# A mixture-of-experts stage on one core: each expert's weights in one transfer in place of two

## The reference

```python
x = x + xattn(layernorm(x), ctx_2048, ...)
h = layernorm(x)
w, sel = top_4(softmax(h @ gate_w.T))          # w made to sum to 1
cw_large[t, sel] += w;  cw_small[t, sel // 2] += w
large = sum_e (silu(h @ Wg[e]) * (h @ Wu[e]) * cw_large[:, e]) @ Wd[e]
small = the same with cWg, cWu, cWd, cw_small
x = x + large + 0.05 * small
```

## Time and profile before

| | |
|---|---|
| median of 3 runs | 1032.56 us (1029.6 to 1033.31) |
| the profiled execution | 1028.99 us, its span 1027.2 us |
| PE busy | 973.1 us, 95% of the span |
| DVE, ACT, POOL busy | 551.2, 313.3 and 299.5 us |
| down product y_ps (L1695) | 213.7 us |
| gate and up, g_ps and u_ps (L1678) | 183.2 and 181.4 us |
| adds into out_x (L1531) | 124.9 us on POOL |
| bytes moved | 168.51 MB, mean 164 GB/s |
| granted clock of PE, mean | 0.977 of full speed |

### The profile page before, as it was taken

How to read it: one execution, slowest core, us unless ns; L and a number is a source line. 1 busy time by engine, 2 the same in 40 slices (tenths; PEclk the granted TensorE clock), 3 DMA queues, 4 the chain that set the end, 5 groups by cost and what they waited for, 6 DMA issues and landing times.

```text
span 1027.2 us, 18902 instructions
## 1 busy us (share of the span) xinstructions
PE 973.1 (95%) x5188; PEld 624.8 (61%) x5189; DVE 551.2 (54%) x1382; ACT 313.3 (31%) x632; POOL 299.5 (29%) x397
## 2 busy tenths in 40 slices
PE   8789999999999898489999999999999999999995
PEld 6557676676666555356666666666666666666662
DVE  5677777777767736944443434444443444444341
ACT  2245455555545554921111111111111111111111
POOL 3011101010111001233444344343444434343433
PEclk9999999999999999669999999999999999999998
DMA  6163144241323017348887998989888899889654
GB/s 225 38 170 79 59 103 104 65 111 56 89 68 94 25 48 292 129 101 201 223 237 184 273 249 222 254 219 254 211 216 222 224 244 262 217 213 258 129 110 83
DMA packets 102683, 168.51 MB, mean 164 GB/s; under 512 B 15536, under 2 KB 65840, under 8 KB 98288
## 3 DMA queue, kind: packets, MB, share of 16 engines
q1 hardware_dynamic: 36624, 103.11, 31.6%
q0 software_dynamic: 17872, 43.58, 22.8%
q10 hardware_dynamic: 48144, 21.25, 7.6%
HBM read 101.56 MB, written 29.36 MB: 127 GB/s over the span
## 4 chain that ended last, share of the span: by engine, by line
PE 55%; DMA 1%; issue 0%; ACTq 0%; ACT 0%; POOL 0%; DVE 0%; POOLq 0%
PE y_ps L1695 19%; PE g_ps L1678 17%; PE u_ps L1678 16%; PE at_ps L1687 2%; DMA out_x<-yb,yidx 0%; DMA xg<-xd,tok 0%; ACTq L1557 0%; POOL out_x L1531 0%; PE xt_ps L1663 0%; ACT yb L1568 0%; ACT xT L1578 0%; ACT sg L1562 0%; DVE a L1631 0%; DVE a L1633 0%; POOLq L1539 0%
## 5 line engine op out<-in xcount | busy, mean ns | idle before, releaser
L1695 PE MATMUL y_ps<-W,aT 128*128 x468 | 213.7, 592 | 0.2 <-issue 0.2
L1531 POOL DMA_INDIRECT out_x<-yb,yidx x78 | 124.9, 1601 | 252.7 <-ACT yb L1568 129.5
L519 DVE TENSOR_REDUCE mx<-s 128x2 f32<-128x512 f32 x256 | 163.4, 682 | 59.2 <-PE s L710 58.5
L1678 PE MATMUL g_ps<-W,xT 128*128 x624 | 183.2, 437 | 0.9 <-ACT xT L1578 0.9
L398 ACT ACTIVATE pt<-stp 128x512 f32<-128x512 f32 x256 | 139.0, 596 | 142.0 <-PE stp L724 141.3
L1678 PE MATMUL u_ps<-W,xT 128*128 x624 | 181.4, 434 | 0.0
L1678 PEld LDWEIGHTS u_ps<-W,xT 128*128 128x128 f32 x624 | 119.1, 191 | 49.9 <-issue 0.8
L1695 PEld LDWEIGHTS y_ps<-W,aT 128*128 128x128 f32 x468 | 88.8, 190 | 87.2 <-issue 75.1
L1678 PEld LDWEIGHTS g_ps<-W,xT 128*128 128x128 f32 x624 | 113.5, 192 | 39.0 <-issue 2.4
L1562 ACT ACTIVATE sg<-g_ps 128x320 f32<-128x320 f32 x78 | 34.1, 438 | 291.1 <-PE u_ps L1678 291.1
L1597 DVE COPY aT<-at_ps 128x384 f32<-128x384 f32 x78 | 43.5, 558 | 137.3 <-PE at_ps L1687 137.3
(11 more groups left out here) (210 smaller groups left out, 898.1 us busy)
## 6 DMA issues: line engine op xcount, KB each, us to landing
W<-in_wts SPq DMA_DIRECT2D x32, 1280.0 KB, 7.9
W<-in_wts SPq DMA_DIRECT2D x32, 768.0 KB, 5.7
stage<-xb ACTq DMA_DIRECT2D x320, 64.0 KB
qst<-q SPq DMA_DIRECT2D x42, 256.0 KB, 5.0
xs<-in_x SPq DMA_DIRECT2D x8, 512.0 KB, 3.7
ctxT<-in_ctx SPq DMA_DIRECT2D x8, 512.0 KB, 4.1
out_x<-xs SPq DMA_DIRECT2D x16, 256.0 KB, 2.2
kst<-k SPq DMA_DIRECT2D x48, 64.0 KB, 2.3
```

Of the source, the lines that this page charges most:

```text
L519: dve.tensor_reduce(mx[j // CH % 2][:, h:2 * G:G], s1[r][:, :, :], AX.X, ALU.max)\
L1531: pool.indirect_dma_start(out[:, :], bass.IndirectOffsetOnAxis(yidx[p][:, :], 0), yb[p][:, :], None, compute_op=ALU.add).then_inc(y_added, ...
L1678: m = pe.matmul(ps_[p][:, 0:IW], xT[p][:, c, :], W[:, bass.ds(buf, 1), (2 * c + g) * IW:(2 * c + g + 1) * IW] .rearrange("p a f -> p (a f) ...
L1695: m = pe.matmul(y_ps[:, :], aT[p][:, c, :], W[:, bass.ds(buf, 1), GW + c * D:GW + (c + 1) * D].rearrange("p a d -> p (a d)"), start=(c == ...
```

## The change

`PIECES` has one entry, the whole row, so a call of `load_piece` moves all 4096 columns, 2 MB. In `route` SP issues four loads where it issued eight. In `experts` the wait for one slot more and the second load are gone: the whole row is loaded when the expert that had the buffer is done. A load raises `w_loaded` by 16, so the wait for an expert is for 16 per use of a buffer, where it was 32. Nothing else differs.

```diff
-PIECES = ((0, GW), (GW, WW))
+PIECES = ((0, WW),)
...
         def _(sp):
-            for n in range(2):
-                load_piece(sp, wts, W, w_loaded, 0, 0, n)
+            load_piece(sp, wts, W, w_loaded, 0, 0, 0)
...
             for p in range(1, NW):
-                for n in range(2):
-                    load_piece(sp, wts, W, w_loaded, 0, p, n)
+                load_piece(sp, wts, W, w_loaded, 0, p, 0)
...
             def arrived(i, p):
-                sp.wait_ge(w_loaded[p], i * (2 * DMA) + 2 * DMA)
+                sp.wait_ge(w_loaded[p], i * DMA + DMA)
                 sp.sem_inc(experts_ready, 1)
...
                     last = sp.value_load(cum_i[0:1, bass.ds(i * NW + p - NW, 1)], min_val=1, max_val=NS)
                     sp.wait_ge(slots_done, last)
                     load_piece(sp, wts, W, w_loaded, i, p, 0)
-                    sp.wait_ge(slots_done, last + 1)
-                    load_piece(sp, wts, W, w_loaded, i, p, 1)
                     arrived(i if p else i - 1, (p - 1) % NW)
```

## The result

| | before | after |
|---|---|---|
| median | 1032.89 us (1029.6 to 1033.31) | 1059.86 us (1048.23 to 1061.99) |
| ratio | | 1.0258, 95% interval 1.0209 to 1.0306 |
| profiled execution | 1028.99 us, span 1027.2 | 1058.70 us, span 1057.0 |
| first down product to last | 461.2 to 1014.5 us | 466.0 to 1044.1 us |

What follows compares the result with a forecast made beforehand. PE was taken to set the stage's time alone. All terms summed to 0, giving 1028.99 us for an execution like the profiled one and an unchanged median of 1032.5 us, range 1028.5 to 1038.

Steps and rivals of the forecast that it cites:

- What bounds the kernel: In the loop over expert slots PE sets the time alone, 7.21 us per slot; everything else has slack.
- SyncE's instructions: 32 of 64 load issues and 28 waits on SyncE go, with only loads queued behind them: gain 0.
- the first four experts: Their 8 MB, loaded ahead of the stage, go in 4 transfers instead of 8: cost 0, some 25 us of cover.
- PE's speed beside traffic: PE's matmuls in the stage average 432 ns over slots with and without loads: price 0.
- The size of a load: A 2 MB load in the stage lands in 9.8 us, lower end 7.9, upper end 13.5: 0 on PE.
- The adds: Serial adds into out_x on GpSimd: the one behind a load lands in 9.0 us, upper end 12.8; price 0.
- The rival of the adds: In the stage the adds into out_x become the bound, 1.1 us lost per gap of two slots: 1039.5 us, chance 6%.
- The gathers: VectorE reads a gather 11.9 us after its issue, 13.7 with its idle time, enough beside a 2 MB load: price 0.
- The moves of x: Moves through the stage buffer may land 11.3 us after their last issue; expected 5.8 us beside the load: price 0.
- that rival fell: The load starves the moves into the stage buffer, PE loses 2.2 us per load, 62 us in all: 1094, chance 4%.
- The range: Forecast median 1028.5 to 1036.5 us from the runs' spread, upper end extended to 1038 for small forms of the adds' case.

Runs made afterwards that it cites:

- the full loads and cheap writes: The changed kernel with its accumulating writes into the output made plain indirect writes, all waits kept: 1030.92 us, ratio 1.0012.
- for the first four: The kernel before the change with only the loads of the first four experts, ahead of the stage, made single: 1029.20 us, ratio 0.9991.
- the mid-slot kernel: The changed kernel with its single 2 MB load issued 4.6 us later in the slot, tied to PE's gate and up products: 1054.37 us, ratio 1.0249.

## Why the prediction was wrong, point by point

- *What bounds the kernel* was right: PE alone, with everything else hidden. The claim that the rest had slack was tested for each stream by itself, at one place of the trace, and that wasn't enough for the chain of adds.
- *SyncE's instructions, the first four experts, PE's speed beside traffic*: 0, 0 and 0, and the runs agree (1.0012 with the full loads and cheap writes, 0.9991 for the first four).
- *The size of a load*: 9.8 us were taken, 10.5 measured. Small, and the wrong way.
- *The adds* are the step that failed, the claim that their lateness can't build up. The 9.0 us for the add behind a load were nearly right: on time, 1.7 us behind the load, it landed in 8.4 to 9.05. But then I let a late add find less of the load before it, by one add beside a 1280 KB piece, and concluded: "A chain whose lateness is set by the load's end can't build up". The runs show that it does. The add of 572.90, 3.0 us behind its load in place of 1.7, took 9.4 us, not less. So a gap of two slots left the chain 15.7 - 14.4 = 1.3 us later than it found it. My own sum had this number, 1.1 us per gap, and put it aside. The second thing I had at nothing is the load behind. My sample was a gap of three slots, with no load at 723.8. In a gap of two, 17 of the 27 (I had counted 16), the next load is issued there, 3.0 us behind the add due at 720.8, and that would still be harmless: the add of 567.05 has a load issued 2.8 us after it and takes 5.0. One more gap of two, with 1.3 us of lateness and 0.3 us of a longer landing, brings the distance to the 1.2 us of 583.12, where the add is held for 10.5. A late add doesn't find less of the load before it, and it finds the load behind it. That sentence was false, and it had kept the right rival at 6%.
- *The rival of the adds* named the mechanism, and its time, 1039.5, was too low. Its 15.5 us for a gap of two are right until the first add meets the next load (15.7 measured); from there it is 17.0. And it had no price for the clock that falls behind a stall of PE, 6.3 of the 24.8 us. Its gaps of three do win time back: the three adds from 616.39 on took 20.4 us, and the next was issued at 636.80. There are 9 of them, and one gap of four, where I had counted 11 of three.
- *The gathers* got 11.9 us of cover at their usual place. I left out that they are queued on GpSimd behind the add: of the 17.0 us of idle time in PE's groups above, 12.8 came by them and only 4.2 by the copy of y that I had watched.
- *The moves of x* were late at times (10.9 us of waits on VectorE, 1.6 at most), within their cover: that rival fell.
- *The range* held only a mild case of that rival. The hint was in the rows: the earlier trace rows give 7.1 and 4.9, with two times 0.8 that is 13.6 of 14.4 us. A serial chain 94% full in gaps of two wasn't slack to be spent.

## What to carry to other kernels

A hidden serial chain of transfers is a second bound: add up its round trips over the shortest spacing at which the disturbance returns, and treat anything that lengthens one of them by more than what is left as a loss. When a transfer is late, look also at what is issued behind it and what is queued behind it on its own engine. Cutting a large background load into pieces a slot apart kept this chain alive, with 1280 and 768 KB as with 1024 and 1024.

## What the runs showed of the hardware

- An accumulating write issued just ahead of a 2 MB load is held as long as one issued behind it: 10.5 us to land at 0.9 us ahead (490.46 in the mid-slot kernel) and at 1.2 us (583.12 after). Issued 1.6 us ahead or more it lands in 4.6 to 5.6, as with no load near.
- Being late behind the load doesn't help much either: 9.05 us at 1.7 us behind it (557.17), 9.4 at 3.0 (572.90).
- A wait of PE can cost more than its length: 4.04 us of idle time were followed by a granted clock of 0.50 and 2.9 us of slower matmuls. A wait of 2.54 us also had slower matmuls behind it (eight g_ps in 3.44 us), one of 2.67 had not (2.34).
- Near the edge the time is not one number: 1536 and 512 KB gave 1030 and 1046 us with the same program.
